# Sums of squares in an attention stage: a pairwise sum split in two rounded parts, fp32r products between keys and queries, and all values copied by ScalarE

## The reference, cut to what matters

```python
def _rmsnorm(x):
    return x * rsqrt(mean(x * x, axis=-1, keepdims=True) + EPS)

def _ada_rmsnorm(x, t, gamma_w, beta_w):
    return (t @ gamma_w.T)[:, None, :] * _rmsnorm(x) + (t @ beta_w.T)[:, None, :]

x = x + a_alpha * _attention(_ada_rmsnorm(x, ...), W_q, W_k, W_v, W_o)   # 16 heads of 16
x = x + f_alpha * _swiglu(_ada_rmsnorm(x, ...), gate_w, hidden_w, out_w, out_b)
```

## Time and profile before

| | |
|---|---|
| median of 3 runs | 787.47 us (787.05 to 789.38) |
| profiled execution | 786.93 us, span 785.0 us |
| granted TensorE clock, mean | 0.992 |
| TensorE busy | 758.4 us, 97% |
| VectorE busy | 525.7 us, 67% |
| GpSimd busy | 402.6 us, 51% |
| ScalarE busy | 353.6 us, 45% |
| squares L1069 | 64 records for 16 tiles |

### The profile page before, as it was taken

How to read it: one execution, slowest core, us unless ns; L and a number is a source line. 1 busy time by engine, 2 the same in 40 slices (tenths; PEclk the granted TensorE clock), 3 DMA queues, 4 the chain that set the end, 5 groups by cost and what they waited for, 6 DMA issues and landing times.

```text
span 785.0 us, 18921 instructions
## 1 busy us (share of the span) xinstructions
PE 758.4 (97%) x6804; PEld 612.0 (78%) x6804; DVE 525.7 (67%) x772; ACT 353.6 (45%) x675; POOL 402.6 (51%) x403
## 2 busy tenths in 40 slices
PE   8999999999997899999999999999999999999994
PEld 7788888888887899999988666767676767787872
DVE  3877877777888888889974554545454555444674
ACT  4344344444457677888773224322232323232343
POOL 4656555655777888988883513131313131001475
PEclk9999999999999999999999999999999999999997
DMA  8955444444431100000004466767675758498352
GB/s 248 265 102 101 102 114 114 106 107 115 107 63 37 44 3 2 0 0 0 3 15 108 138 185 178 223 177 226 174 227 172 229 170 231 132 338 306 140 190 108
DMA packets 79559, 103.95 MB, mean 132 GB/s; under 512 B 39280, under 2 KB 52816, under 8 KB 79376
## 3 DMA queue, kind: packets, MB, share of 16 engines
q1 hardware_dynamic: 76912, 98.99, 44.5%
q10 hardware_dynamic: 2592, 4.20, 1.4%
HBM read 73.52 MB, written 21.25 MB: 121 GB/s over the span
## 4 chain that ended last, share of the span: by engine, by line
PE 84%; POOL 5%; issue 3%; DVE 3%; DMA 2%; ACT 1%; SPq 1%; POOLq 0%; ACTq 0%; DVEq 0%
PE banks L1111 23%; PE banks L434 21%; PE banks L1125 12%; PE banks L965 5%; PE banks L1145 4%; PE banks L451 3%; PE banks L1040 3%; PE banks L998 3%; PE banks L1080 3%; PE banks L1022 2%; PE banks L1056 2%; DMA early<-in_cond_w 2%; PE banks L1069 1%; POOL sums L1669 1%; POOL x_sb L1675 1%
## 5 line engine op out<-in xcount | busy, mean ns | idle before, releaser
L1457 DVE TENSOR_TENSOR g<-banks,silu 128x512 f32<-128x512 f32 x64 | 44.2, 691 | 109.6 <-ACT silu L1326 62.3
L1326 ACT ACTIVATE silu<-banks 128x512 f32<-128x512 f32 x64 | 38.3, 598 | 110.6 <-PE banks L1111 110.6
L1460 DVE TENSOR_TENSOR g_lo<-g,g_hi 128x512 fp32r<-128x512 f32 x64 | 53.9, 842 | 45.9 <-ACT g_hi L1332 45.9
L434 PE MATMUL banks<-up_hi,xs_hi 128*128 128x512 f32 x256 | 82.2, 402 | 2.1 <-POOL xs_lo L363 1.5
L1332 ACT ACTIVATE g_hi<-g 128x512 fp32r<-128x512 f32 x64 | 40.5, 632 | 96.4 <-DVE g L1457 95.3
L1111 PE MATMUL banks<-mlp_in_hi,w_hi 128*128 128x512 f32 x256 | 80.5, 396 | 0.1
L1111 PE MATMUL banks<-mlp_in_lo,w_hi 128*128 128x512 f32 x256 | 79.9, 393 | 0.0
L1111 PE MATMUL banks<-mlp_in_hi,w_lo 128*128 128x512 f32 x256 | 79.8, 393 | 0.0
L434 PE MATMUL banks<-up_lo,xs_hi 128*128 128x512 f32 x256 | 79.4, 391 | 0.1
L434 PE MATMUL banks<-up_hi,xs_lo 128*128 128x512 f32 x256 | 79.2, 391 | 0.0
L723 POOL TENSOR_TENSOR mlp_in_lo<-mlp_in,mlp_in_hi 128x1024 fp32r<-128x1024 f32 x8 | 23.2, 2900 | 96.7 <-ACT mlp_in_hi L730 96.7
(11 more groups left out here) (188 smaller groups left out, 1821.4 us busy)
## 6 DMA issues: line engine op xcount, KB each, us to landing
gen_hyper<-in_gen_t SPq DMA_DIRECT2D x32, 512.0 KB, 4.8
gen_made<-base_w SPq DMA_DIRECT2D x64, 256.0 KB, 3.9
adapter_w<-gen_made SPq DMA_DIRECT2D x64, 256.0 KB, 3.5
tokens<-in_x_tok SPq DMA_DIRECT2D x32, 128.0 KB, 2.5
w_stage<-in_w_t SPq DMA_DIRECT2D x32, 128.0 KB, 2.4
tokens_again<-in_x_tok SPq DMA_DIRECT2D x32, 128.0 KB, 2.2
weight_slot<-adapter_w SPq DMA_DIRECT2D x4, 1024.0 KB, 8.8
w_hi<-adapter_w SPq DMA_DIRECT2D x4, 1024.0 KB, 5.6
```

The costliest lines, as they stand in the source:

```text
L434: last = nc.tensor.matmul(bank[2 * j + part][:, :], (xs_hi, xs_lo)[a][:, k, d, :], up[b][:, d, at:at + 512], start=n == d == 0, stop=n == ...
L1326: nc.scalar.activation(silu[:, f % 2, :], bank[2 * (f % 2)][:, :], ACT.Silu).then_inc(S["silu_done"], 1)
L1457: nc.vector.tensor_tensor(g[:, f % 2, :], bank[2 * (f % 2) + 1][:, :], silu[:, f % 2, :], ALU.mult).then_inc(S["g_done"], 1)
L1460: nc.vector.tensor_tensor(gs[1][:, f % 2, :], g[:, f % 2, :], gs[0][:, f % 2, :].bitcast(FP32), ALU.subtract).then_inc(S["g_ready"], 1)
```

## The change

The squares of the two halves are added on VectorE (squares_sum), the sum is rounded to fp32r on ScalarE (squares_high), the rest is taken on VectorE (squares_low), and TensorE multiplies a rounded matrix of ones with the low and the high part, two fp32r products in place of two fp32 ones. The last three tiles keep the fp32 products. Both parts take the memory of the squares, in place. On TensorE the squares move behind the keys; on ScalarE the root's Ln and Exp move ahead of the query copy. ScalarE copies all four quarters of the values, except in the first two value steps and the last, where VectorE keeps its two. GpSimd makes the rounded ones once.

```diff
+            with ExitStack() as cq:
+                sq_parts = sb("sq_parts", [P, DH, GTA], FP32R, cq)
             sq = sb("sq1", [P, DH, GTA], within=ca)
...
+        def vector_takes_values(s):
+            return s.first_tile(2) or s.first_tile(3) or s.last(2)
...
+            pool.wait_ge(Z["ones_done"], 1)
+            nc.gpsimd.tensor_copy(core["ones_r"][:], core["ones"][:]).then_inc(A["ones_done"], 1)
...
             def squares(s):
                 if s.live(5):
+                    split = not isinstance(s.at(5), int) or s.at(5) < NA - LATE
                     ps = bank[5 if s.last(3) else 4 if s.last(4) or s.last(5) else 3]
-                    pe.wait_ge(A["sq_done"], s.at(5) + 1)
+                    if s.first_tile(5):
+                        pe.wait_ge(A["ones_done"], 1)
+                    pe.wait_ge(A["sq_ready" if split else "sq_done"], s.at(5) + 1)
...
-                    for d in range(DH):
-                        last = nc.tensor.matmul(ps[:, 0:GTA], core["ones"][:], sq[:, d, :], start=d == 0, stop=d == DH - 1)
+                    for n in range(2):
+                        last = nc.tensor.matmul(ps[:, 0:GTA], (core["ones_r"] if split else core["ones"])[:],
+                                                sq_parts[:, 1 - n, :] if split else sq[:, n, :], start=n == 0, stop=n == 1)
...
+                keys(s)
                 squares(s)
-                keys(s)
                 queries(s)
...
+                    if not vector_takes_values(s):
+                        nc.scalar.activation(value_slots(s, 1, 0), value_sums(s, 1, 0), ACT.Copy)
+                        nc.scalar.activation(value_slots(s, 1, 1), value_sums(s, 1, 1), ACT.Copy).then_inc(A["v_high_done"], 1)
...
+            def squares_high(s):
+                if s.live(5):
+                    act.wait_ge(A["sq_sum_done"], s.at(5) + 1)
+                    nc.scalar.activation(sq_parts[:, 1, :], sq[:, 0, :], ACT.Copy).then_inc(A["sq_hi_done"], 1)
...
                 take_values(s)
+                squares_high(s)
...
+                rstd(s)
                 take_queries(s)
                 output_high(s)
...
-                rstd(s)
                 square(s)
...
             take_values(d1)
+            squares_high(d1)
...
+            def squares_sum(s):
+                if s.live(5):
+                    ve.wait_ge(A["sq_done"], s.at(5) + 1)
+                    nc.vector.tensor_tensor(sq[:, 0, :], sq[:, 0, :], sq[:, 1, :], ALU.add).then_inc(A["sq_sum_done"], 1)
+
+            def squares_low(s):
+                if s.live(5):
+                    ve.wait_ge(A["sq_hi_done"], s.at(5) + 1)
+                    nc.vector.tensor_tensor(sq_parts[:, 0, :], sq[:, 0, :], sq_parts[:, 1, :].bitcast(FP32),
+                                            ALU.subtract).then_inc(A["sq_ready"], 1)
...
             def attention_body(s):
-                take_values(s)
+                if vector_takes_values(s):
+                    take_values(s)
+                squares_sum(s)
                 maxima(s, 0)
+                squares_low(s)
                 maxima(s, 1)
```

More of the change, by code:

```diff
@@ L140, in program @@
         core["stat_loaded"] = ctx.enter_context(nc.semaphore("stat_loaded"))
+        core["ones_r"] = sb("ones_r", [P, P], FP32R)
         core["rows"] = [sb("row_squares", [P, T // P]), sb("row_rstd", [P, 4])]
@@ L788, in layers @@
                  "s_ready max_done sub_done exp_done sum_done rec_done norm_done pt_ready pt_done pv_ready ot_hi_done "
-                 "ot_done o_ready ya_done x_done sq_done ss_ready ss_ln_done ss_done base_loaded base_done base_stored").split()
+                 "ot_done o_ready ya_done x_done sq_done sq_sum_done sq_hi_done sq_ready ones_done ss_ready ss_ln_done ss_done base_loaded base_done base_stored").split()
         A = {n: sem("a_" + n) for n in names} | core["att_sems"]
```

## The result

The changed kernel takes 795.66 us (median of 4 runs, 793.64 to 798.05) where the kernel before takes 787.26 (4 runs, 786.70 to 789.38): 1.0096 times as long, 95% interval 1.0070 to 1.0123. It is slower by 5.5 to 9.7 us. The profiled execution took 794.55 us, 7.62 more than that of before (786.93); its span is 792.6.

A forecast was written before the change was run, and what follows sets the result against it. TensorE was taken to bound the attention stage, GpSimd's own loop 0.06 us behind, VectorE third in lockstep. Ten periods 6.15, first squares_sum 0.3 and step 16 2.4 make 8.85 us on 786.93: 795.8 us, range 788.5 to 807.0.

The forecast's parts named there:

- squares_sum: VectorE addition, waiting for GpSimd's second product with the reciprocals: about 1.4 us instead of 0.42, ending 0.3 us behind it.
- squares_low: VectorE subtraction, slipping into GpSimd's gap ahead of its third input product: 0.4 us per tile, with 0.15 us margin.
- TensorE and ScalarE: TensorE saves 0.62 us per tile, at most 0.06 usable; ScalarE's added 1.1 us fits into 2.06 us of room.
- The period, 11.28 for 11.4: Attention loop, steps 6 to 16: ten tiles at 11.4 us against 10.785, 6.15 us more.
- The first squares_sum at step 5: Start of the loop: the first squares_sum was charged 0.3 us.
- Step 16: Near the loop's end: squares_low waits 1.65 us for a GpSimd instruction; the way to the next reciprocal product grows 2.4 us.
- g + 2.7: When squares_low is ready, in us after g, the end of GpSimd's second product with the reciprocals.
- Behind it: After step 16: GpSimd's low part releases TensorE's first hidden product; nothing changes behind that, 0 us.
- A longer wait: Rival: squares_low misses its gap, or GpSimd's waiting L181 precedes squares_sum; about 1.05 us per tile, 806 us; chance 0.20.
- No exclusion: Rival: both VectorE additions find the port free or are too short to hold GpSimd; 786.4 us; chance 0.12.
- A cheaper port: Rival: squares_sum lands between two GpSimd instructions and costs only its own 0.42 us; 789 to 792 us; chance 0.17.
- A gain: Rival: a measurable gain, needing GpSimd's loop to be shorter than the 10.76 us it shows; chance 0.03.

The follow-up runs named there:

- e2: Kernel before with ScalarE rounding the squares itself and fp32r products for the same 13 tiles, low part left out, nothing added on VectorE: 786.78 us, ratio 0.9985.
- e5: e1 without squares_low; TensorE takes the high part of the sum alone, in one product: 788.97 us, ratio 1.0000.
- e7: Kernel before with only the value copies changed, all four on ScalarE from step 4 to 16: 787.34 us, ratio 0.9992.
- e4: Changed kernel with two of the four value copies back on VectorE, ahead of squares_sum: 800.02 us, ratio 1.0132.
- e1: Changed kernel with squares_sum made by one reduction over the pair, into a tile of its own: 794.35 us, ratio 1.0074.
- e10: Kernel before with GpSimd's first product of the next tile's input made in its gap waiting for ScalarE's rounding copy: 785.74 us, ratio 0.9979.
- e3: Changed kernel with ScalarE's Ln and Exp back behind the rounding of the output, as before: 794.86 us, ratio 1.0071.
- e12: Changed kernel with GpSimd's gap filled as in e10: 799.01 us, ratio 1.0151.
- e8: e1 with squares_low after both pairs' maxima and TensorE's squares' product behind the queries: 791.73 us, ratio 1.0047.
- e11: Kernel before with GpSimd's gap filled as in e10 and the fp32r products of e2, low part left out: 778.15 us, ratio 0.9876.
- e6: Changed kernel with two unused reciprocals on VectorE ahead of squares_low, to delay it: 811.97 us, one run.
- e9: e8 with GpSimd's gap filled as in e10, all parts of the product kept: 784.93 us, ratio 0.9965.

## Why the prediction was right, and where it was not

It said 795.8 us and slower; measured were 795.66 and slower by 0.96%. The mechanism is the one that it named; that the two times agree within 0.2 us is luck. It charged the attention stretch with 8.85 us, and the stretch grew by 6.07; in the profiled execution the 2.18 us at the start, which the change didn't cause, made up for most of the difference. Point by point, in the order of its steps:

*TensorE and ScalarE.* The saving of 0.62 us per tile is there (0.86 to 0.24 us) and brings nothing by itself: e2. GpSimd's loop is 10.73 us by e2 and e5, where 10.76 was read. ScalarE's additions are 0.38 twice and 0.42, 1.18 us for the predicted 1.1, and hidden: e7, e5. That the idle time of TensorE would be 0.6 + 0.6 us per tile was too much: 6.43 us in the 8.6 periods of the stretch is 0.75.

*squares_sum.* 1.40 us for "about 1.4", ending 0.28 us behind L898, as forecast; GpSimd gives up 0.20 us (1.48), where the prediction had 0.14.

*squares_low.* In its gap, 0.41 us, for 0.42. The margin ahead of L188 was 338.82 - 338.56 = 0.26 us rather than 0.15.

*The period, 11.28 for 11.4: a mis-sized term.* Measured against the prediction's steps: L898's end to the maxima 0.20 for 0.3, and the maxima to the reciprocal's end 7.20 for 7.28. In both places I added an instruction's full recorded time, but on VectorE the next row starts 0.08 us before the recorded end of the last (336.17 against 336.25; 338.89 against 338.97). That makes 0.18 on a sum of 11.44, which the prediction wrote as 11.4; over ten tiles 4.93 us were paid of the 6.15 charged.

*The first squares_sum at step 5: 0.3 charged, nothing paid* (-0.08 to step 6). Both additions waited there (1.36 and 0.98 us), but the engines were not yet in lockstep: TensorE was idle for 6.5 of before's 36.32 us up to step 6, which absorbed it.

*Step 16: 2.4 charged, 0.60 paid.* The step that failed is "just behind the start of L717". The prediction has squares_low 0.25 us behind it (g + 2.7 against g + 2.45). squares_low came 2.38 us after the maxima, as said, but L718 started 0.20 us later than I had it: L714 in front of it had itself been held by squares_sum's handover and took 2.58 us, not 2.38. I had let that handover delay L181 but forgot it for L713, which stands in its place. That alone would have left squares_low behind by 0.05 us; it also came 0.07 us earlier than I had it (2.63 us behind L714's start, not 2.7), and that turned the order. So squares_low was first, by 0.02 us, and the 1.65 us fell away (L718 itself took 2.16 us instead of 1.91, inside its slack ahead of L907). In e4, where the order is turned by 0.11 us, the wait comes: 1.66.

*Behind it: 0 charged, 0.62 paid.* I had put the hidden product's release with GpSimd's low part, which ended at 401.43. That was one of three ends in before, and not the last:

```profile
400.37 1.10 PE L1056 MATMUL banks<-pt_sb,v_sb 128*32 128x64 f32 x64 [0.25 <-ACT pt_sb L1231]
400.77 0.68 DVE L1440 TENSOR_TENSOR y_alpha<-banks,cond_vectors 128x512 f32<-128x512 f32 x1
```

The weighted values on TensorE itself ended at 401.47 and VectorE's scaled output at 401.45, so the three stood within 0.04 us of each other. In step 17 squares_sum and squares_low run once more on VectorE, 0.84 us by their records, ahead of the scaled output; that made the scaled output the last release (409.77 against 409.25), 0.52 us behind the low part. The prediction listed what is moved in step 16 and not the same two instructions one step further.

*The 2.18 us at the start were in no sum*, and are no part of the change: they are a longer wait for a load and the lower clock behind it, as shown above. The traces of e1, e2 and e5 have the same, with waits of 1.98, 1.54 and 2.09 us and the clock at 0.50 for 3.41 to 6.83 us, and reach the first product with the reciprocals at 243.02 to 245.79 us. The ten others, e10 with 3.41 us of the lower clock at 14.41 among them, reach it at 240.71 to 241.86, e3, almost the same kernel as after, at 241.10. Why TensorE waits longer for the load in some executions stays open, as each kernel has one trace. So the size of the change itself is the stretch's 6.07 us, near e3's 5.6 and at the lower end of the measured interval. Against it the prediction's 8.85 had 1.2 us too much in the periods, 0.4 in the first tile and 1.2 at the end (2.4 for 0.60 + 0.62). That nothing changes behind the hidden product held: the difference stayed between 8.1 and 8.5 us for the next 320 us.

*The rivals.* "A longer wait" didn't come in after, but it lay close: 0.26 us of margin in each tile, and e12 shows its price, 0.9 us per tile. Its other half, that GpSimd's ready L181 goes ahead of the waiting squares_sum, is out: in steps 6 to 15 of after L182 followed squares_sum each time. "No exclusion" is out: the waits show in every trace that has squares_low. "A cheaper port" is what e8 is, 791.73 us, by other code. A gain was not to be had while GpSimd's loop stood at 10.73; e11 shows what it took to get one.

## What to carry to other kernels

Where two engines' loops are within a tenth of a microsecond of each other, work taken off one brings next to nothing until the other's loop is shortened too: ask first for the second loop, and try the two cuts together (each alone gave 0.09 and 0.00 us per tile here, both together 0.62). A VectorE instruction that reads two tensors from SBUF beside a busy GpSimd had no fixed price in these runs: it cost its own time where it landed between two GpSimd instructions and the rest of the running one where it didn't; so either give it another form, such as a reduction over the pair, or place it in a gap that GpSimd has anyway, with a margin. Follow such an instruction into the last steps too, where the neighbours are twice as wide and another engine's result may become the last release.

## What the runs showed of the hardware that was not expected

*The handover is sharp, and constant.* A waiting VectorE instruction of 128x256 ended 0.27 to 0.29 us behind the recorded end of the GpSimd instruction that it waited for, in eight places: after 336.25 (L898 ends 335.97), e1 340.17 (339.88), e3 334.16 (333.89), e4 279.96 (279.67) and 398.89 (398.61), e6 332.29 (332.00), e9 342.23 (341.94), e12 339.22 (338.94). Where GpSimd's next instruction was ready at once, it was held back by 0.20 us (L182, 1.28 to 1.48, in after and e3); where 0.19 us or more lay between the two, as in e1, it wasn't (1.04). In after L182 was ready behind L898 in each of steps 6 to 15 and never got in ahead of the squares_sum that was waiting.

*Hundredths decide.* Who starts first goes through: squares_low took 0.41 us where it was 0.02 us ahead of GpSimd's instruction, in after (394.93 against 394.95), and 2.60 us where it was 0.02 us behind, in e1 (406.57 against 406.55). The wait then lasts as long as the neighbour, so a change of 0.1 us anywhere earlier on either engine can turn into one of 1 to 2 us.

*Removing a wait can move the next instruction into one.* e1 took 0.71 us of squares_sum's 1.40 away, and squares_low, now earlier in GpSimd's cycle, paid 0.48 of it back.
